# The last graph layer of four: its linear products kept in SBUF up to the output, a degree factor moved into the edge sums

## The chip, the cores and the metric

The kernel is one program on one core of a Trainium2 chip. The metric is the device time of that program in microseconds, from launch to the last output row in memory. Five instruction streams run side by side on the core and meet only through semaphores: TensorE (PE), VectorE (DVE), ScalarE (ACT), GpSimd (POOL) and SyncE (SP), which here does nothing but issue DMA transfers.

## What is computed

Four graph layers on 10,000 nodes of 512 features and 5,000 edges sorted by target: a GIN layer, a SAGE layer, a two-layer attention block and a GCN layer. Each is followed by a residual sum and a layer normalisation. The change is in the fourth, apart from two small tables that are made earlier.

```python
def _gcn_conv(x, edge_index, W, b):
    xw = x @ W.T
    deg = ...                      # edges into the node, plus its own loop
    dinv = rsqrt(deg)
    norm = dinv[row] * dinv[col]   # source times target
    out = segment_sum(norm[:, None] * xw[row], col)
    return out + b

identity = x
h = _gcn_conv(x, edge_index, W, b)
h = _batch_norm(h, gamma, beta)    # mean and variance of each feature over all nodes
h = gelu(h)
x3_out = h + identity
x = _layernorm(x + x3_out, axis=-1)
```

The batch norm needs statistics over all nodes, so no row of the output can be made before the last row of `h` has been seen. Since both `dinv[col]` and the loop belong to the target, the input of the product for node n is `dinv[n] * (sum over its edges of dinv[src] * x[src] + dinv[n] * x[n])`.

## The kernel before

The nodes are padded to 10,240 and taken in 20 groups of 512, each group as four subtiles of 128 rows. The program is a row of stages. At the end of each stage all five engines meet at a barrier (`Kernel.run`, lines 284 to 288), so that a stage lasts as long as its slowest engine and its slowest awaited transfer. The last four stages are:

1. **Edge sums** (`edge_sum_stage`, line 952). The 40 tiles of 128 edges are gathered by POOL (line 987), multiplied on PE by a mask whose entries carry the source's factor (lines 1033 and 1056), and copied out of PSUM by ACT into one of three buffers (line 1047, or line 1045 where `out_scale` is given). SP stores each tile's sums and picks two of their rows for sums that run across tiles (lines 1005 to 1007). ACT waits until the buffer's three transfers of three tiles ago have landed.
2. **Linear stage** (`linear_stage(kn, "gcn")`, line 1660). SP loads the group's rows of x3 into `l_x`, POOL gathers its edge sums into `l_z`. DVE makes `x * dinv + sum` (line 1753) and multiplies the result by `dinv` once more (line 1758). PE turns it feature by feature (line 1820), ACT and DVE split it into two float16 parts (lines 1789 and 1765), and PE makes four products `mm[m]` of 12 matmuls each with the weights' two parts (`split_product`, lines 320 to 322). ACT adds the bias (line 1801) into `l_h`, DVE takes batch norm statistics of it (line 1779), and SP stores the group's `l_h`, 1 MB, in the scratch tensor `h` in memory (line 1710). The turns of the next group stand ahead of products m = 2 and m = 3 (`turns`, line 1671), with two PSUM banks for them.
3. **Coefficients** (`norm_coefficients_stage`, line 1844): aggregates the statistics (line 1856) into one scale and shift for each feature.
4. **Batch norm stage** (`batch_norm_stage(kn, "gcn")`, line 1876). SP loads the group's `h` again into `b_h` (line 1924), 1 MB, and its x3 into `b_x` (line 1928), 1 MB. ACT applies scale, shift and Gelu (line 2023), PE turns the result back to rows (line 2067), DVE forms `2 * x + turned` (line 1984) with layer norm statistics (lines 1425 and 1428), POOL makes the reciprocal root (lines 1434 and 1437), DVE applies it into `b_o` (line 1445), and SP stores 1 MB of output rows (line 1935). All buffers are in pairs.

The loops of stages 2 and 4 are hardware loops over pairs of groups, with the last pair written out behind the loop (`in_pairs`, line 131). Stage 1 is straight-line code. The order on each engine is the order in which the code is written. The order on SP in stage 4 is, for each group, load of h, load of x, wait for the group's output rows, store.

Whoever reads the code: `kn.w_hi` and `kn.w_lo` hold all layers' weights in SBUF, 13 units of 2,048 float16 columns and a few more, in each of 128 partitions. The last unit (`W_GCN`) is the GCN layer's. The others, the masks `kn.apart` and two bias tiles have been read for the last time when stage 2 begins.

## Time and profile before

| | us |
|---|---|
| median of three runs | 4247.26 |
| fastest and slowest of them | 4243.65 and 4253.40 |
| the profiled execution, its own time | 4247.18 |
| the profiled execution, its span | 4245.5 |
| edge sums of the last layer, first to last instruction | 3627 to 3723 |
| linear stage | 3725 to 4012.5 |
| coefficients | 4016 to 4020.6 |
| batch norm stage | 4020.7 to 4245.5 |

The span is from the first to the last instruction of the profiled execution; 1.68 us of its own time lie outside it. Over the whole program PE is busy 84%, PE's weight loads 51%, DVE 51%, ACT 34% and POOL 34% of the span. These shares hide that the stages have different limits: PE is busy 94% of the linear stage and 32% of the batch norm stage. The reader should take times of the trace as microseconds from the span's start, and "idle" as time in which an engine stood before the named instruction.

### The profile page before, as it was taken

Reading aid. Unit: us, or ns where it says so; the run is one execution under the profiler, and the core shown is the slowest. Engines: PE = TensorE matmul, PEld = TensorE weight load, DVE = VectorE, ACT = ScalarE, POOL = GpSimd, SP = SyncE. Lnnn points to the kernel's source line nnn. Section 1 sums busy time; section 2 is a strip of 40 time slices with the busy share of each in tenths; the row PEclk is TensorE's granted clock in tenths of the full one; section 3 lists DMA queues with packets and bytes.
Section 4 is the critical chain, followed back from the end, with each engine's and each line's share of the span. In section 5 each row is a group of like instructions: output and inputs, shape, how many; then the busy total and the mean of one; then the engine's idle time right before and its main releaser. Section 6 shows DMA issues by size and latency. Waiting matters only on the chain. (4 is left out here: it accounts for less than half of the span.)

```text
span 4245.5 us, 59057 instructions
## 1 busy us (share of the span) xinstructions
PE 3572.1 (84%) x20056; PEld 2145.6 (51%) x20056; DVE 2165.2 (51%) x4085; ACT 1429.8 (34%) x2512; POOL 1455.5 (34%) x1188
## 2 busy tenths in 40 slices
PE   4589994599997999987599999998859999679733
PEld 3134441255554777765366666666635555234422
DVE  7167776433333444446643424213757887057576
ACT  1333333222222444344233323222534443323332
POOL 2455543322211222243433333213446665333111
PEclk7799996799998999999799999999979999789955
DMA  1767766543433556577876676744867675657587
GB/s 66 225 176 199 200 168 229 176 141 119 136 111 143 209 209 225 191 219 220 244 204 201 196 205 196 207 110 149 265 225 268 248 267 185 207 199 238 203 278 276
DMA packets 554428, 841.83 MB, mean 198 GB/s; under 512 B 288134, under 2 KB 288134, under 8 KB 552272
## 3 DMA queue, kind: packets, MB, share of 16 engines
q1 hardware_dynamic: 487120, 619.31, 44.4%
q0 software_dynamic: 67200, 221.25, 17.7%
q8 instruction: 47, 0.77, 0.1%
q14 instruction: 61, 0.50, 0.0%
HBM read 491.80 MB, written 284.56 MB: 183 GB/s over the span
## 5 line engine op out<-in xcount | busy, mean ns | idle before, releaser
L321 PE MATMUL bank<-w_lo,t_r_hi 128*128 128x344 f16 (+1 forms) x2560 | 837.1, 327 | 0.0
L322 PE MATMUL bank<-w_hi,t_r_hi 128*128 128x344 f16 (+1 forms) x2560 | 836.9, 327 | 0.0
L320 PE MATMUL bank<-w_hi,w_lo 128*128 128x344 f16 (+1 forms) x1280 | 418.7, 327 | 30.7 <-DMA w_lo<-g_row_lo 30.7
L2237 DVE SCALAR_TENSOR_TENSOR t_z<-w_lo,t_z 128x256 f32<-128x256 f32 x320 | 205.9, 704 | 440.3 <-DMA w_lo<-h 437.8
L320 PE MATMUL bank<-l_z_hi,w_lo 128*128 128x512 f16 x960 | 365.3, 381 | 1.5 <-DVE l_z_lo L1765 1.5
L321 PE MATMUL bank<-l_z_lo,w_hi 128*128 128x512 f16 x960 | 365.3, 380 | 0.0
L322 PE MATMUL bank<-l_z_hi,w_hi 128*128 128x512 f16 x960 | 365.0, 380 | 0.0
L2211 POOL TENSOR_TENSOR t_row_lo<-t_r,t_row_hi 128x1024 f16<-128x1024 f32 x80 | 181.3, 2267 | 517.0 <-ACT t_row_hi L2258 516.8
L1456 POOL DMA_INDIRECT l_z<-sum,slot_i x160 | 160.6, 1004 | 519.5 <-PE bank L1820 436.7
L320 PE MATMUL bank<-w_hi 128*128 128x344 f16 x960 | 297.7, 310 | 45.5 <-DMA w_hi<-t_row_lo 45.5
L322 PEld LDWEIGHTS bank<-w_hi,t_r_hi 128*128 128x128 f16 x2560 | 250.9, 98 | 168.3 <-issue 0.3
L321 PEld LDWEIGHTS bank<-w_lo,t_r_hi 128*128 128x128 f16 x2560 | 250.8, 98 | 162.1 <-issue 0.2
L1779 DVE BATCH_NORM_STATS2 bn_stats<-l_h 128x512 f32 (+2 forms) x160 | 107.1, 679 | 415.0 <-ACT l_h L1801 365.0
L320 PE MATMUL bank<-w_hi,b_z_lo 128*128 128x344 f16 x960 | 297.2, 310 | 0.0
L321 PE MATMUL bank<-w_lo,b_z_hi 128*128 128x344 f16 x960 | 297.1, 309 | 0.0
L322 PE MATMUL bank<-w_hi,b_z_hi 128*128 128x344 f16 x960 | 297.0, 309 | 0.0
L1056 PE MATMUL bank<-e_rows,e_lhs 128*128 128x512 f32 x240 | 164.9, 819 | 146.2 <-ACT e_out L1045 49.7
L2269 ACT ACTIVATE w_hi<-bank 128x344 f32<-128x344 f32 x240 | 109.1, 456 | 516.6 <-PE bank L322 516.6
L1801 ACT ACTIVATE l_h<-bank,vec 128x512 f32<-128x512 f32 x160 | 109.9, 687 | 507.4 <-PE bank L322 471.3
L2067 PE MATMUL bank<-ident,b_h 128*128 128x128 f32 x640 | 115.6, 349 | 169.3 <-ACT b_h L2023 167.2
L320 PE MATMUL bank<-w_hi,t_r_lo 128*128 128x512 f16 x640 | 242.8, 379 | 0.0
L2413 POOL TENSOR_TENSOR t_r_lo<-t_r,t_r_hi 128x512 f16<-128x512 f32 x160 | 196.3, 1235 | 96.4 <-ACT t_r_hi L2481 89.6
(277 smaller groups left out, 7031.7 us busy)
## 6 DMA issues: line engine op xcount, KB each, us to landing
w_lo<-h SPq DMA_DIRECT2D x160, 512.0 KB
h<-b_wide SPq DMA_DIRECT2D x80, 516.0 KB, 3.0
...
```

The costliest lines, as they stand in the source:

```text
L320: pe.matmul(out, s_lo, m_hi, start=(k == 0), stop=False)
L321: pe.matmul(out, s_hi, m_lo, start=False, stop=False)
L322: mm = pe.matmul(out, s_hi, m_hi, start=False, stop=last)
L1056: pe.matmul(total[t % 2][:], lhs[t % L][:], rows[t % W][:], start=True, stop=True).then_inc(summed.sem, 1)
L1456: pool.indirect_dma_start(out, None, sums, bass.IndirectOffsetOnAxis(ap=kn.slot_i[:, g * S + s:g * S + s + 1], axis=0), bounds_check=kn.d. ...
L1779: v.bn_stats(kn.bn_stats[:, m, ds(g * 6, 6)], h[u][:, m, 0:real]).then_inc(seen.sem, 1)
L1801: act.activation(h[u][:, m, :], mm[m][:], ACT.Identity, scale=UNSCALE, bias=kn.vec[:, bias + m:bias + m + 1]).then_inc(h_done.sem, 1)
L2067: ins = pe.transpose(tp[u][s][:, m * P:(m + 1) * P], h[u][:, m, s * P:(s + 1) * P], kn.ident[:])
L2211: nc.gpsimd.tensor_tensor(row_lo[:, s, :], r_f[s % 2][:], row_hi[:, s, :], ALU.subtract)\
L2237: ins = v.scalar_tensor_tensor(out=z[u][:, s, cols], in0=hrow[:, s, cols], scalar=z[u][:, s, HC + h:HC + h + 1], in1=z[u][:, s, cols], op0 ...
L2269: act.activation(wide[s % 2][:, third * THIRD:(third + 1) * THIRD], mm[s % 2][third], ACT.Copy, scale=UNSCALE).then_inc(wide_done.sem, 1)
L2413: g_.tensor_tensor(r_lo[:, u, k, :], r_f[k % 2][:], r_hi[:, u, k, :], ALU.subtract)\
```

## The change

The batch norm stage of the last layer no longer reads its input back from memory. A new class `Held` names 80 places of 128 by 512 float32 in SBUF, four for each group: 48 in the room of the used weights, 5 in the masks', 2 in the bias tiles', 17 new buffers, and for the last two groups the two input buffers `l_x`. `gcn_stage` takes the place of `linear_stage(kn, "gcn")`. ACT writes each product with its bias to its place, and nothing is stored. It has four PSUM banks for turned rows, all four turns of the next group stand ahead of product m = 1, and DVE scales the input of group g + 2 ahead of the statistics of product m = 2 of group g. DVE's second pass over the input is gone. For this the edge sums of the last layer are multiplied by the target's factor while they leave PSUM (`out_scale`, and `rim_dinv` for sums that cross tiles), and the node's own row by the squared factor `node_scale`. DVE makes the two degrees in the setup, and POOL makes three small tables of them at the end of the second layer's linear stage.

`output_stage` takes the place of `batch_norm_stage(kn, "gcn")`. ACT applies Gelu in place. Only x3 is loaded, four groups ahead, into four own buffers and then into the room of held groups that have been turned and read (`held.whole`). DVE's sum is written over x in place, and ACT instead of DVE applies the layer norm, in place, with a shift that POOL makes in two more small operations. The output is stored from there. Both new stages are straight-line code.

```diff
@@ -709,11 +714,13 @@
         dve.wait_ge(own, n)
         n = st.mark(v.tensor_scalar(alike[:], alike[:], 1.0, None, ALU.add))
         dve.wait_ge(own, n)
+        v.tensor_tensor(kn.dst_dinv[:], alike[:], inside[:], ALU.add).then_inc(tables.degrees.sem, 1)
         st.mark(v.reciprocal(kn.mean_scale[:], alike[:]))
         dve.wait_ge(products.sem, products.at(RIM_COUNTED))
         st.mark(v.tensor_scalar(rim_f[0:T, 4:5], rim_count_ps, -1.0, float(T * P), ALU.mult, ALU.add))
         n = st.sig.at(st.first + st.n)
         dve.wait_ge(own, n)
+        v.tensor_scalar(kn.rim_dinv[0:T, :], rim_f[0:T, 4:5], 1.0, None, ALU.add).then_inc(tables.degrees.sem, 1)
         st.mark(v.reciprocal(kn.rim_mean_scale[0:T, :], rim_f[0:T, 4:5]))
         v.memset(kn.bn_stats[:], 0.0)
         slots(dve)
@@ -1738,7 +1745,13 @@
         if sage:
             pool.wait_ge(dinv_in.sem, dinv_in.at(16 * d.tiles))
             nc.gpsimd.tensor_scalar(kn.src_dinv_neg[:], kn.src_dinv[:], -1.0, None, ALU.mult).then_inc(negated.sem, 1)
-            pool.wait_ge(negated.sem, negated.at(1))
+            nc.gpsimd.tensor_tensor(kn.dst_dinv[:], kn.dst_dinv[:], kn.minus_half[:, 0:d.tiles], ALU.pow)\
+                .then_inc(negated.sem, 1)
+            nc.gpsimd.tensor_tensor(kn.rim_dinv[0:d.tiles, :], kn.rim_dinv[0:d.tiles, :],
+                                    kn.minus_half[0:d.tiles, 0:1], ALU.pow).then_inc(negated.sem, 1)
+            nc.gpsimd.tensor_tensor(kn.node_scale[:], kn.node_dinv[:], kn.node_dinv[:], ALU.mult)\
+                .then_inc(negated.sem, 1)
+            pool.wait_ge(negated.sem, negated.at(4))
 
     def vector(dve):
         v = nc.vector
+class Held:
+    def __init__(self, kn, mem):
+        d = kn.d
+        room = []
+        for w in (kn.w_hi, kn.w_lo):
+            free = w[:, 0:kn.unit_at(W_GCN)].bitcast(F32)
+            room += [free[:, n * D:(n + 1) * D] for n in range(kn.unit_at(W_GCN) // (2 * D))]
+        free = kn.apart[:].rearrange("p t q -> p (t q)").bitcast(F32)
+        room += [free[:, n * D:(n + 1) * D] for n in range(d.tiles * P // (2 * D))]
+        room += [kn.gin_b2[:], kn.fc_b[:]]
+        self.x = [kn.buffer(mem, f"l_x{u}", [P, S, D], F32) for u in range(2)]
+        room += [kn.buffer(mem, f"held{n}", [P, D], F32)[:] for n in range((d.groups - 2) * 4 - len(room))]
+        room = room[:(d.groups - 2) * 4] + [self.x[u][:, m, :] for u in range(2) for m in range(4)]
+        self.rows = [room[g * 4:g * 4 + 4] for g in range(d.groups)]
+        self.whole = [w[:, n * 8 * D:(n + 1) * 8 * D].bitcast(F32).rearrange("p (s c) -> p s c", s=S)
+                      for w in (kn.w_hi, kn.w_lo) for n in range(kn.unit_at(W_GCN) // (8 * D))]
+def gcn_stage(kn, held):
...
+    tp = [kn.bank[n] for n in (0, 1, 6, 7)]
+    mm = [kn.bank[2 + n] for n in range(4)]
...
+    def sync(sp):
+        for g in range(G):
+            i, u = divmod(g, 2)
+            if g >= 2:
+                sp.wait_ge(z_ready.sem, z_ready.at((g - 1) * S))
+            sp.dma_start(x[u][:], node_rows(dram["x3"], i, u)).then_inc(x_in[u].sem, 16)
+    def gpsimd(pool):
+        for g in range(G):
+            i, u = divmod(g, 2)
+            if g >= 2:
+                pool.wait_ge(turned.sem, turned.at((g - 1) * 4))
+            for s in range(S):
+                gather_sums(kn, pool, z[u][:, s, :], dram["sum"], g, s, sum_in[u])
+    def vector(dve):
+        v = nc.vector
+        def scale(g):
+            i, u = divmod(g, 2)
+            dve.wait_ge(x_in[u].sem, x_in[u].at(i * 16 + 16))
+            dve.wait_ge(sum_in[u].sem, sum_in[u].at(16 * S * (i + 1)))
+            for s in range(S):
+                own = kn.node_scale[:, g * S + s:g * S + s + 1]
+                v.scalar_tensor_tensor(out=z[u][:, s, :], in0=x[u][:, s, :], scalar=own,
+                                       in1=z[u][:, s, :], op0=ALU.mult, op1=ALU.add).then_inc(z_ready.sem, 1)
+        def low_parts(g):
+            u = g % 2
+            for k in range(4):
+                dve.wait_ge(hi_done.sem, hi_done.at(g * 4 + k + 1))
+                v.scalar_tensor_tensor(out=z_lo[u][:, k, :], in0=tp[k][:], scalar=A_SCALE, in1=z_hi[u][:, k, :],
+                                       op0=ALU.mult, op1=ALU.subtract).then_inc(lo_done.sem, 1)
+        scale(0)
+        low_parts(0)
+        scale(1)
+        for g in range(G):
+            for m in range(4):
+                if m == 1 and g + 1 < G:
+                    low_parts(g + 1)
+                if m == 2 and g + 2 < G:
+                    scale(g + 2)
+                dve.wait_ge(h_done.sem, h_done.at(g * 4 + m + 1))
+                v.bn_stats(kn.bn_stats[:, m, g * 6:(g + 1) * 6], held.rows[g][m][:, 0:real(g)]).then_inc(seen.sem, 1)
+        dve.wait_ge(seen.sem, seen.at(4 * G))
+    def scalar(act):
+        def high_parts(g):
+            u = g % 2
+            for k in range(4):
+                act.wait_ge(turned.sem, turned.at(g * 4 + k + 1))
+                act.activation(z_hi[u][:, k, :], tp[k][:], ACT.Copy, scale=A_SCALE).then_inc(hi_done.sem, 1)
+        high_parts(0)
+        for g in range(G):
+            for m in range(4):
+                if g + 1 < G and m == 1:
+                    high_parts(g + 1)
+                own = held.rows[g][m]
+                act.wait_ge(mid.sem, mid.at(g * 4 + m + 1))
+                act.activation(own, mm[m][:], ACT.Identity, scale=UNSCALE,
+                               bias=kn.vec[:, V_GCN_B + m:V_GCN_B + m + 1]).then_inc(h_done.sem, 1)
+    def tensor(pe):
+        def turn(g):
+            u = g % 2
+            pe.wait_ge(z_ready.sem, z_ready.at(g * S + S))
+            for k in range(4):
+                pe.wait_ge(lo_done.sem, lo_done.at((g - 1) * 4 + k + 1))
+                for s in range(S):
+                    ins = pe.transpose(tp[k][:, s * P:(s + 1) * P], z[u][:, s, k * P:(k + 1) * P], kn.ident[:])
+                ins.then_inc(turned.sem, 1)
+        turn(0)
+        for g in range(G):
+            u = g % 2
+            pe.wait_ge(lo_done.sem, lo_done.at(g * 4 + 4))
+            for m in range(4):
+                if g + 1 < G and m == 1:
+                    turn(g + 1)
+                pe.wait_ge(h_done.sem, h_done.at((g - 1) * 4 + m + 1))
...
...
+def output_stage(kn, held):
...
+    own = [kn.buffer(mem, f"o_x{b}", [P, S, D], F32)[:] for b in range(B)]
+    x = (own + held.whole + own)[:B + len(held.whole)] + own
...
+    tp = [kn.bank[0:4], kn.bank[4:8]]
...
+    def sync(sp):
+        def load(g):
+            if g >= B:
+                sp.wait_ge(y_done.sem, y_done.at((g - B) * S + S))
+            if g >= B + len(held.whole):
+                sp.wait_ge(first_stored.sem, first_stored.at(16 * B))
+            sp.dma_start(x[g], node_rows(dram["x3"], *divmod(g, 2))).then_inc(x_in[g % B].sem, 16)
...
+            sp.wait_ge(rows_out.sem, rows_out.at(g * S + S))
+            sp.dma_start(node_rows(dram["out"], *divmod(g, 2)), x[g])\
+                .then_inc((first_stored if g < B else stored).sem, 16)
+        sp.wait_ge(first_stored.sem, first_stored.at(16 * B))
+        sp.wait_ge(stored.sem, stored.at(16 * (G - B)))
+    def gpsimd(pool):
+        for g in range(G):
+            i, u = divmod(g, 2)
+            if g >= 2:
+                pool.wait_ge(rows_out.sem, rows_out.at((g - 1) * S))
+            norm.pool(pool, i, u)
+            pool.wait_ge(norm.rstd.sem, norm.rstd.at(g * 2 + 2))
+            nc.gpsimd.tensor_tensor(shift[:, u, :], norm.moments[:, u, :, 0], norm.power[:, u, :], ALU.mult)\
+                .then_inc(shifted.sem, 1)
+            pool.wait_ge(shifted.sem, shifted.at(g * 2 + 1))
+            nc.gpsimd.tensor_scalar(shift[:, u, :], shift[:, u, :], -1.0, None, ALU.mult).then_inc(shifted.sem, 1)
+    def vector(dve):
+        v = nc.vector
+        for g in range(G):
+            i, u = divmod(g, 2)
+            b = g % B
+            dve.wait_ge(x_in[b].sem, x_in[b].at(16 * (g // B + 1)))
+            if g >= 2:
+                dve.wait_ge(rows_out.sem, rows_out.at((g - 1) * S))
+            for s in range(S):
+                dve.wait_ge(rows_turned.sem, rows_turned.at(g * S + s + 1))
+                v.scalar_tensor_tensor(out=x[g][:, s, :], in0=x[g][:, s, :], scalar=2.0, in1=tp[u][s][:],
+                                       op0=ALU.mult, op1=ALU.add).then_inc(y_done.sem, 1)
+                dve.wait_ge(y_done.sem, y_done.at(g * S + s + 1))
+                norm.moments_of(dve, x[g][:, s, :], s, i, u)
+    def scalar(act):
+        def apply(g):
+            for m in range(4):
+                own = held.rows[g][m]
+                act.activation(own, own, ACT.Gelu, scale=kn.bn_scale[:, m:m + 1],
+                               bias=kn.bn_shift[:, m:m + 1]).then_inc(f_done.sem, 1)
+        apply(0)
+        apply(1)
+        for g in range(G):
+            u = g % 2
+            if g + 2 < G:
+                apply(g + 2)
+            act.wait_ge(shifted.sem, shifted.at(g * 2 + 2))
+            for s in range(S):
+                act.activation(x[g][:, s, :], x[g][:, s, :], ACT.Identity, scale=norm.power[:, u, s:s + 1],
+                               bias=shift[:, u, s:s + 1]).then_inc(rows_out.sem, 1)
+    def tensor(pe):
+        for g in range(G):
+            u = g % 2
+            pe.wait_ge(f_done.sem, f_done.at(g * 4 + 4))
+            for s in range(S):
+                pe.wait_ge(y_done.sem, y_done.at((g - 2) * S + s + 1))
+                for m in range(4):
+                    ins = pe.transpose(tp[u][s][:, m * P:(m + 1) * P], held.rows[g][m][:, s * P:(s + 1) * P],
+                                       kn.ident[:])
+                ins.then_inc(rows_turned.sem, 1)
...
 def graph_layers_kernel(nc, nodes, edges, io):
     d = Dims(nodes, edges)
     dram = dict(io)
@@ -2578,10 +2837,12 @@
         kn.add(edge_attention_stage(kn, dram["h2"]))
         kn.add(gat_stage(kn, 2))
         with ExitStack() as mem:
-            kn.add(edge_sum_stage(kn, mem, dram["x3"], (kn.src_dinv, kn.src_dinv_neg), None, None))
-        kn.add(linear_stage(kn, "gcn"))
-        kn.add(norm_coefficients_stage(kn, V_GCN_G, V_GCN_BETA))
-        kn.add(batch_norm_stage(kn, "gcn"))
+            kn.add(edge_sum_stage(kn, mem, dram["x3"], (kn.src_dinv, kn.src_dinv_neg), kn.dst_dinv, kn.rim_dinv))
+        with ExitStack() as mem:
+            held = Held(kn, mem)
+            kn.add(gcn_stage(kn, held))
+            kn.add(norm_coefficients_stage(kn, V_GCN_G, V_GCN_BETA))
+            kn.add(output_stage(kn, held))
         kn.run()
```

DVE's rows of the last two groups in the linear stage, before, behind the loop. `l_z` is the input, `l_z_lo` its low part, `bn_stats` the statistics, and `l_h_247` and `l_h_248` the two groups' products:

```order
L1753 SCALAR_TENSOR_TENSOR l_z_244<-l_x_242,node_dinv,l_z_244 128x512 x4
L1758 TENSOR_SCALAR l_z_244<-l_z_244,node_dinv 128x512 x4
L1779 BN_STATS bn_stats<-l_h_247 128x6 x2
L1765 SCALAR_TENSOR_TENSOR l_z_lo<-bank,l_z_hi 128x512 x2
L1779 BN_STATS bn_stats<-l_h_247 128x6
L1765 SCALAR_TENSOR_TENSOR l_z_lo<-bank,l_z_hi 128x512 x2
L1779 BN_STATS bn_stats<-l_h_247 128x6
L1779 BN_STATS bn_stats<-l_h_248 128x6 x4
```

The same engine now, two groups in the middle of the new stage:

```order
L2633 SCALAR_TENSOR_TENSOR l_z_lo_265<-bank,l_z_hi_263 128x512 x4
L2646 BN_STATS bn_stats<-w_hi 128x6
L2626 SCALAR_TENSOR_TENSOR l_z_260<-l_x_241,node_scale,l_z_260 128x512 x4
L2646 BN_STATS bn_stats<-w_hi 128x6 x3
L2633 SCALAR_TENSOR_TENSOR l_z_lo_264<-bank,l_z_hi_262 128x512 x4
L2646 BN_STATS bn_stats<-w_hi 128x6
L2626 SCALAR_TENSOR_TENSOR l_z_261<-l_x_242,node_scale,l_z_261 128x512 x4
L2646 BN_STATS bn_stats<-w_hi 128x6 x3
```

The scaling of a group stood directly ahead of the low parts of the same group, in two passes. It is now one pass, and the low parts of another group and four statistics stand between a group's scaling and its own low parts.

ACT's rows at the start of the last stage, before (`b_h` is the reloaded h). The branch closes the loop:

```order
L2023 ACT_TABLE_LOAD
L2023 ACTIVATE b_h_252<-b_h_252,bn_shift,bn_scale 128x512 x4
L2023 ACTIVATE b_h_253<-b_h_253,bn_shift,bn_scale 128x512 x4
L134 REGISTER_ALU
L134 COMPARE_AND_BRANCH
```

And now, where `w_hi` is room of held products, and `o_x_269` and `o_x_270` are the first two groups' output rows:

```order
L2767 ACT_TABLE_LOAD
L2767 ACTIVATE w_hi<-w_hi,bn_shift,bn_scale 128x512 x12
L2778 ACTIVATE o_x_269<-o_x_269,o_shift,n_power 128x512 x4
L2767 ACTIVATE w_hi<-w_hi,bn_shift,bn_scale 128x512 x4
L2778 ACTIVATE o_x_270<-o_x_270,o_shift,n_power 128x512 x4
```

Gelu of three groups now stands ahead of the first layer norm on ACT, and one group's Gelu stands between each two layer norms. There is one table load in front of all of them.

## Rows read from the trace of the kernel before

**Rows 1.** Busy time by window; columns: window, length, PE, PEld, DVE, ACT, POOL, PEclk, DMA, GB/s.
```profile
3627.00:3720.00 93.00, 55.43 (x81) 17.77 (x82) 0.00 (x0) 38.91 (x80) 39.98 (x40) 0.74 0.75 239
3747.50:4012.50 265.00, 247.28 (x1264) 127.51 (x1264) 180.67 (x309) 93.96 (x156) 72.41 (x72) 0.99 0.65 218
4020.70:4245.50 224.80, 71.15 (x320) 63.86 (x320) 158.34 (x320) 70.08 (x89) 30.97 (x40) 0.58 0.81 280
...
4000.00:4011.00 11.00, 11.00 (x52) 4.80 (x49) 2.03 (x4) 2.75 (x4) 0.00 (x0) 1.00 0.25 95
...
3450.00:3500.00 50.00, 50.00 (x265) 26.66 (x263) 40.27 (x66) 20.29 (x32) 31.28 (x30) 1.00 0.72 260
```

**Rows 2.** Waits in the last stage, 4050 to 4200: total us, times, longest.
```profile
ACT b_h L2023 <- DMA b_h<-h: 102.7, 14, 13.1
```

**Rows 3.** Waits of PE in the linear stage, 3760 to 4011.
```profile
PE bank L1820 <- DVE l_z L1758: 16.0, 18, 0.9
```

**Rows 4.** Timeline of PE around one of these waits; start, duration, what, idle before.
```profile
3965.95 0.38 PE L322 MATMUL bank<-l_z_hi,w_hi 128*128 128x512 f16 x1
3967.25 1.09 PE L1820 MATMUL bank<-ident,l_z 128*128 128x128 f32 x8 [0.92 <-DVE l_z L1758]
```

**Rows 5.** Timeline of DVE: the second pass, in the first group and at that wait.
```profile
3739.98 1.68 DVE L1758 TENSOR_SCALAR l_z<-l_z,node_dinv 128x512 f32<-128x512 f32 x4
...
3965.43 1.67 DVE L1758 TENSOR_SCALAR l_z<-l_z,node_dinv 128x512 f32<-128x512 f32 x4
```

**Rows 6.** Timeline of DVE at the end of the linear stage.
```profile
4011.81 0.45 DVE L1779 BATCH_NORM_STATS2 bn_stats<-l_h 128x6 f32<-128x272 f32 x1 [2.15 <-ACT l_h L1801]
4016.12 2.36 DVE L1856 BATCH_NORM_AGGREGATE c_mv<-bn_stats 128x2 f32<-128x120 f32 x4 [3.87 <-SPq L287]
```

**Rows 7.** Timeline at the start of the last stage.
```profile
4020.82 1.28 ACT L2023 ACT_TABLE_LOAD   x1 [9.05 <-DVEq L287]
...
4026.19 2.93 ACT L2023 ACTIVATE b_h<-b_h,bn_shift,bn_scale 128x512 f32<-128x512 f32 x4 [4.08 <-DMA b_h<-h]
4029.25 3.67 PE L2067 MATMUL bank<-ident,b_h 128*128 128x128 f32 x16 [18.20 <-ACT b_h L2023]
4030.50 0.69 DVE L1984 SCALAR_TENSOR_TENSOR b_y<-b_x,bank 128x512 f32<-128x512 f32 x1 [9.90 <-PE bank L2067]
```

**Rows 8.** Timeline of DVE: subtiles of one group in the last stage.
```profile
4165.39 0.69 DVE L1984 SCALAR_TENSOR_TENSOR b_y<-b_x,bank 128x512 f32<-128x512 f32 x1 [3.72 <-PE bank L2067]
...
4167.06 0.69 DVE L1984 SCALAR_TENSOR_TENSOR b_y<-b_x,bank 128x512 f32<-128x512 f32 x1
...
4172.18 1.92 DVE L1445 TENSOR_SCALAR b_o<-b_y,n_moments,n_power 128x512 f32<-128x512 f32 x4
```

**Rows 9.** DMA in the last stage: its mean over 4050 to 4200, and one window.
```profile
DMA packets 22262, 44.21 MB, mean 295 GB/s; under 512 B 676, under 2 KB 676, under 8 KB 22262
...
4051.00:4062.00 11.00, 3.59 (x16) 3.27 (x16) 6.62 (x15) 4.21 (x5) 1.75 (x2) 0.55 1.03 366
```

**Rows 10.** Timeline at the end of the program.
```profile
4235.40 0.18 DVE L1428 BATCH_NORM_AGGREGATE n_moments<-n_stats 128x2 f32<-128x6 f32 x1
...
4236.19 1.27 POOL L1437 TENSOR_TENSOR n_power<-n_power,minus_half 128x4 f32<-128x4 f32 x1
4237.58 1.91 DVE L1445 TENSOR_SCALAR b_o<-b_y,n_moments,n_power 128x512 f32<-128x512 f32 x4 [0.15 <-POOL n_power L1437]
```

**Rows 11.** Lines 1045 and 1047 (min, median, max ns), and waits in 3627 to 3722.
```profile
L1045 ACT ACTIVATE e_out<-bank,mean_scale x40: 675/687/688, 686.0 to 788.3; 128x512 f32<-128x512 f32 x40
...
L1047 ACT COPY e_out<-bank x80: 572/585/586, 110.2 to 3714.3; 128x512 f32<-128x512 f32 x80
...
ACT e_out L1047 <- DMA e_last<-e_out: 30.7, 23, 3.6
```

**Rows 12.** POOL: costliest groups, and its timeline around the SAGE layer's end.
```profile
L531 POOL TENSOR_TENSOR node_dinv<-degree,minus_half 128x80 f32<-128x80 f32 x1 | 13.3, 13319 | 0.1
...
1312.03 0.23 POOL L1868 TENSOR_SCALAR c_rstd<-c_mv 128x4 f32<-128x4 f32 x1 [75.86 <-DVE c_mv L1856]
```

54 lines of the change are left out of this document (53 added, 1 removed).

## The prediction, made before the changed kernel ran

> **What bounds the kernel now.** I read the windows by stage first, since the change touches only the last 620 us of 4245.5 [rows 1]. In the linear stage (265 us from its first product to its end) PE is busy 247 us at a granted clock of 0.99, so PE sets the pace there. In the last stage (224.8 us) PE is busy 71 us, DVE 158, ACT 70, and the DMA engines 0.81 of the time at 280 GB/s. No engine is full there, so I went to the waits. ACT stood 102.7 of 150 us until the reload of h had landed, on 14 of 14 groups [rows 2]. The loop closes through a pair of buffers: the next h is requested when PE has turned the last one, and 3 MB a group (h, x, output) must pass. This costs 224.8 / 20 = 11.2 us a group. In the linear stage the one wait of PE is for DVE's second pass over the input [rows 3].
>
> **Linear stage, steady part.** PE stood 16.0 us in 18 waits, 0.89 us each [rows 3]. In the timeline the last product before such a wait starts at 3965.95 and the turn at 3967.25 [rows 4], while products follow each other every 11.00 / 52 = 0.21 us when nothing waits [rows 1]. So the step takes 1.30 us instead of 0.21, of which 0.92 is counted as idle; about 0.17 more hides under the modelled end of the product. The second pass (1.67 us [rows 5]) ends just before the turn starts. The change removes it and also puts the whole scaling one group earlier on DVE, so the wait should vanish, not shrink: 18 x (0.89 + 0.17) = **19.1 us**. What is late next? A group then takes PE some 12.1 us. DVE's work in it is four scalings, four low parts and four statistics, at about 0.7 us each 8.4 us, ACT's eight operations of 0.6 to 0.7 us some 5.2 us. The new scaling of group g + 2 waits for gathers that POOL issues once group g has been turned, more than a group earlier. If they were late, DVE would hold back statistics, which nothing on PE needs. The four turn banks are freed by low parts of a group before. Nothing is left for PE to wait on. The share of dense work rises; a stretch in which PE was busy 50.00 of 50 us kept a clock of 1.00 [rows 1], so I take no loss of clock.
>
> **Linear stage, its two ends.** The first group's second pass, 1.68 us, lies between its input and the first turn [rows 5]: **1.7 us**. Four banks in place of two may add some tenths, left out. At the end, the last statistics finish at 4012.26, and the aggregation starts only at 4016.12, after 3.87 us of idle that SP's queue ended, the last store of h [rows 6]. That store is gone. A barrier alone takes 0.2 us or so (the last stage's table load starts within that of the coefficients' end), so **3.6 us**. The stores of h elsewhere in the stage cost nothing and give nothing back.
>
> **Last stage, start.** Before, the stage's start at 4020.7 leads over the first landing of h to ACT at 4026.19, PE at 4029.25 and DVE at 4030.50 [rows 7]. Now ACT loads its table (1.28 us, to 4022.10) and has its input at once: four Gelus, 2.93 us, to 4025.05; PE 0.13 later; DVE 1.25 after PE, at 4026.4. The first x is now the first transfer asked for and should land as h did, by 4026.2, just hidden. First DVE operation: 5.7 us after the start of the stage.
>
> **Last stage, pace.** DVE per subtile: 4167.06 - 4165.39 = 1.67 us for sum, statistics and aggregation, with its waits between [rows 8]; four make 6.68 us. The application, 1.92 us a group, leaves DVE. Against this stand: ACT with four Gelus (2.93 us, [rows 7]) and four layer norm applications. The last form is not in the trace for SBUF input; it costs at most what Gelu costs in place, 2.93, and at least what DVE took, 1.92. I take 2.9, near Gelu, since it runs on the same engine with the same two vector operands. ACT is then busy 5.9 us of 6.68. Does its latency fit? After DVE ends a group, POOL's chain takes 1.9 us as before (4235.58 to 4237.46 [rows 10]) and 0.6 us for two more small operations (one such takes 0.23 [rows 12]); ACT's application ends 5.5 us after DVE's end, its Gelu for three groups on 8.4 us after, and PE's turn of 3.7 us at 12.1 us, when DVE needs it at 13.4. It fits with about 1 us over. PE's turns themselves take 3.7 of 6.7 us. DMA moves 2 MB (2.10 million bytes) a group instead of 3: in 6.68 us that is 314 GB/s. The stage's mean was 295 GB/s with ACT waiting for it, but a window of 11 us ran at 366 [rows 9], which would need 5.7 us a group. So DVE becomes the bound: 20 x 6.68 = **133.6 us**.
>
> On DMA, the Trainium skill (DMA: Bandwidth & Descriptors, Specifications) gives a limit of about 358 GB/s between memory and one core. By that figure a group would need at least an estimated 5.9 us, and the sum would stay as it is. The trace's 366 GB/s over 11 us lies slightly above it.
>
> **Last stage, end.** Before, from the last aggregation's end (4235.58) to the span's end (4245.5) passed 9.9 us [rows 10]. POOL's two operations add 0.6, ACT's application in place of DVE's 1.0: 11.5 us. The whole stage is 5.7 + 133.6 + 11.5 = 150.8 us against 224.8: **74.0 us** less.
>
> **Edge sums.** The copy out of PSUM with a factor took 0.687 us against 0.585 without [rows 11], on 40 tiles. If each were on the path, 4.1 us; if none, 0. It cannot gain. SP's queue (three transfers a tile) sets much of the pace, while ACT waited for a landing 23 times [rows 11]; behind such a wait the 0.1 us counts, but the three buffers share it. I take **+1.5 us**, nearer the lower end.
>
> **What should cost nothing.** DVE's two new operations in the setup are on tables of 40 columns, some 0.2 us each, beside edge sums. POOL's power over 80 columns took 13.3 us [rows 12], so the two new powers and a product may take 7 to 8 us. They stand behind POOL's last gather in the SAGE layer, where POOL then idles 75.9 us until the stage's end [rows 12]. Without that cover they would cost those 8 us.
>
> **Sum.** 4247.18 (the profiled execution, 1.68 outside its span) - 19.1 - 1.7 - 3.6 - 74.0 + 1.5 = 4150.3. The median of the three runs is 0.08 higher. I say **4150 us**. Its own range is 4142 to 4156: DVE's subtile may take 1.63 us (3 us less over 80), the edge sums 0 to 4.1 us, the tail and the starts 2 us either way.
>
> **Rivals.**
>
> *DMA sets the last stage's pace.* If loads and stores interleave no better than before, at 295 GB/s [rows 9], a group takes 7.1 us and the stage 8.4 us more: **4159 us**. For it: loads and stores of 1 MB alternate on one queue, and the required 314 GB/s is above the mean of before. Against it: that mean contains times in which nothing was asked for, and loads run four groups ahead. Chance 0.14.
>
> *ACT sets it.* The application now shares an engine and a latency loop with Gelu. If Gelu and the application needed different tables, two loads of 1.28 us would be added: 5.9 + 2.6 = 8.5 us a group, 36 us more, **4186 us**. For it: the trace shows a table load again and again in the last stage. Against it: the order of the changed kernel has a single one, ahead of all groups. A milder form, an application that waits 0.5 us a group longer than I count, gives 4160. Chance 0.07 together.
>
> *The linear stage keeps its wait.* With all turns ahead of one product, high parts, low parts and turns form a chain in one place, and PE may wait there as long as it did: 4169 us. Against it: PE has three products, 7.8 us, behind the turns, and the chain behind them is 2 us long. Chance 0.04.
>
> *Straight-line code starves the engines: slower than before.* Both stages lose their loops. PE gets 960 products and 320 turns in the linear stage as fresh code, with their weight loads. If fetching it made each of these 1,280 pairs wait, the gain of 97 us would be gone at 0.076 us a pair, a pace of 0.29 us instead of 0.21. At 0.1 us a pair the time is 4150 + 128 = **4278 us**. Against it: the last two groups before are already behind the loop, and ran at 0.21 us [rows 1]; that is only 200 pairs or so, so longer streams are not shown. Chance 0.03.
>
> The Trainium skill (Runtime: NRT & Kernel Launch, Instruction fetch mechanics) says that the sequencer prefetches code in order in blocks of 16 KiB, mostly hidden, and that taken branches are what breaks it. By that rule this rival's cost is nothing. No row here shows a long dense stream of new code.
>
> **Chances and range.** Forecast 0.70, DMA 0.14, ACT 0.07, linear wait 0.04, slower 0.03, and 0.02 that some other cost eats the gain to within 0.2% (8 us), which is about what a measurement of this kernel can tell from no change. A range of 4135 to 4170 takes in the forecast, the DMA case, the mild ACT case and the kept linear wait, and some room below for starts that overlap better and subtiles of 1.63 us. Faster by over 0.2%: 0.95; within: 0.02; slower: 0.03.
>
> **What would show it.** In the changed profile: no wait of PE for DVE in the linear stage, and 12.1 us a group there; the aggregation within 0.5 us of the last statistics; DVE in the last stage with 1.67 us a subtile and hardly any idle, ACT waiting for POOL's shift and not for DMA; one table load; DMA near 310 GB/s; the last stage near 151 us, the edge sums 1 to 2 us longer. It would be wrong if DVE's sum waits for `o_x` or `w_hi` transfers (DMA), or for turns that wait for Gelu (ACT), or if PE's products space out beyond 0.22 us (code).

## The result, and the profile after

The changed kernel takes **4139.28 us**, the median of 4 runs (4137.12 to 4144.01), against 4247.23 (4243.65 to 4253.4, 4 runs) for the kernel before on the same chip. The ratio is 0.9746 (95% interval 0.973 to 0.9761): 108 us less. Two later sets of five runs gave medians of 4143.16 and 4140.17, so a single median is good to some 2 to 4 us. The forecast of 4150 with the range 4135 to 4170 held; the gain was 7 to 11 us larger than foretold. The prediction's narrower range for its own forecast, 4142 to 4156, did not take in 4139.28.

The windows of the changed kernel by stage (window, length, busy time of PE, PEld, DVE, ACT, POOL, granted clock, DMA share, GB/s) are: the input of the linear stage, its steady part, the coefficients, the last stage. They answer to [rows 1].

```profile
3721.60:3741.20 19.60, 3.65 (x16) 3.27 (x16) 5.56 (x9) 2.39 (x4) 8.64 (x9) 0.53 0.83 267
3741.20:3982.60 241.40, 240.66 (x1264) 127.56 (x1264) 148.11 (x231) 92.06 (x156) 77.29 (x72) 1.00 0.49 153
3982.60:3987.80 5.20, 0.00 (x0) 0.00 (x0) 3.29 (x8) 1.29 (x2) 1.29 (x2) 0.81 0.01 3
3987.80:4135.10 147.30, 67.79 (x320) 60.93 (x320) 117.29 (x240) 115.08 (x160) 33.37 (x80) 0.59 0.84 285
```

From the first product on PE is busy 240.66 of 241.40 us. Before, it was busy 247.28 of 265.00. The last stage takes 147.3 us instead of 224.8, and ACT is now as full there as DVE. The waits of PE between 3700 and 3960 answer to [rows 3]; the columns are total us, times, longest:

```profile
PE bank L2673 <- DVE l_z L2626: 17.7, 1, 17.7
...
PE bank L324 <- DVE l_z_lo L2633: 1.4, 1, 1.4
```

Both stand at the start of the stage, ahead of the first turn and the first product. No wait of PE follows until the stage's end at 3982.6. The 18 waits of 0.9 us in [rows 3] are gone. The timeline at the seam of the stages (start, duration, what, idle before) answers to [rows 6, 7]:

```profile
3982.63 0.44 DVE L2646 BATCH_NORM_STATS2 bn_stats<-l_x 128x6 f32<-128x272 f32 x1 [2.15 <-ACT l_x L2663]
3983.22 2.36 DVE L1869 BATCH_NORM_AGGREGATE c_mv<-bn_stats 128x2 f32<-128x120 f32 x4
3983.23 1.28 ACT L2767 ACT_TABLE_LOAD   x1 [0.64 <-PEq L291]
...
3987.79 8.57 ACT L2767 ACTIVATE w_hi<-w_hi,bn_shift,bn_scale 128x512 f32<-128x512 f32 x12 [3.28 <-DVEq L291]
3990.82 7.53 PE L2788 MATMUL bank<-ident,w_hi 128*128 128x128 f32 x44 [8.95 <-ACT w_hi L2767]
3993.47 0.69 DVE L2758 SCALAR_TENSOR_TENSOR o_x<-o_x,bank 128x512 f32<-128x512 f32 x1 [5.75 <-DMA o_x<-x]
```

The aggregation follows the last statistics after 0.15 us (3983.22 less 3983.07), where DVE had stood 3.87 us. ACT's table load now comes right behind the linear stage's barrier, 4.5 us ahead of the first Gelu, so it hides under the coefficients; the forecast had it inside the last stage. The first sum still starts 5.7 us after the stage, since its input x now lands last: 3993.47 less 3987.79.

DVE's subtiles in the last stage (answer to [rows 8]) and the waits of 3995 to 4120 (answer to [rows 2]):

```profile
4041.20 0.65 DVE L2758 SCALAR_TENSOR_TENSOR w_hi<-w_hi,bank 128x512 f32<-128x512 f32 x1
4041.88 0.69 DVE L1432 BATCH_NORM_STATS2 n_stats<-w_hi 128x6 f32<-128x512 f32 x1
4042.72 0.18 DVE L1435 BATCH_NORM_AGGREGATE n_moments<-n_stats 128x2 f32<-128x6 f32 x1
4042.82 0.66 DVE L2758 SCALAR_TENSOR_TENSOR w_hi<-w_hi,bank 128x512 f32<-128x512 f32 x1
```

```profile
ACT o_x L2778 <- POOL o_shift L2746: 10.0, 6, 5.8
ACT w_hi L2778 <- POOL o_shift L2746: 5.0, 6, 0.8
ACT w_lo L2778 <- POOL o_shift L2746: 5.0, 6, 0.8
...
DVE n_moments L1435 <- DVE n_stats L1432: 0.3, 2, 0.2
```

No engine waits for a reloaded h or for x. ACT waits 0.8 us a group for POOL's shift, and DVE stands for nothing but its own last result: a period of 1.62 to 1.66 us a subtile. So DVE is the bound, as forecast. Of its 1.62 us only 0.65 + 0.69 + 0.18 = 1.52 are busy as counted; the step from the start of the statistics to the start of the aggregation takes 0.84 us.

### The profile page after: what moved, and what is told of

Its sections match the earlier page's. It is cut to its first block and busy times, and to the rows that moved or that the text cites. A ratio compares the mean times of both kernels' runs of the same rounds, so it can differ in the third digit from the quotient of the medians.

```text
span 4135.1 us, 57582 instructions
## 1 busy us (share of the span) xinstructions
PE 3554.7 (86%) x20056; PEld 2138.1 (52%) x20056; DVE 2089.7 (51%) x3927; ACT 1479.1 (36%) x2584; POOL 1476.6 (36%) x1231
## 5 line engine op out<-in xcount | busy, mean ns | idle before, releaser
L1792 DVE BATCH_NORM_STATS2 bn_stats<-l_h 128x512 f32 (+2 forms) x80 | 54.5, 682 | 337.2 <-ACT l_h L1814 299.6
L2491 ACT ACTIVATE t_r<-bank,vec_scaled 128x512 f32<-128x512 f32 x160 | 109.7, 685 | 293.3 <-PE bank L2522 241.6
L1463 POOL DMA_INDIRECT t_z<-sum_gat,slot_i x160 | 166.2, 1039 | 122.1 <-SPq L291 79.2
```

Of the source, the lines that this page charges most:

```text
L1463: pool.indirect_dma_start(out, None, sums, bass.IndirectOffsetOnAxis(ap=kn.slot_i[:, g * S + s:g * S + s + 1], axis=0), bounds_check=kn.d. ...
L1792: v.bn_stats(kn.bn_stats[:, m, ds(g * 6, 6)], h[u][:, m, 0:real]).then_inc(seen.sem, 1)
L2491: act.activation(r_f[k % 2][:], tp[k % 4][:], ACT.Relu, scale=A_SCALE, bias=kn.vec_scaled[:, bias + k:bias + k + 1]).then_inc(r_done.sem, 1)
```

## The experiments

Each kernel ran beside the kernel before on the same chip (medians there 4244.43, 4244.93 and 4248.45). "Path" is read from each trace: first product to last statistics for the linear stage, first sum to last aggregation for the last stage.

| kernel | median us | ratio, 95% interval |
|---|---|---|
| before, with the degree factors alone | 4219.85 | 0.9938 [0.9921, 0.9955] |
| before, two stages in straight-line code | 4243.8 | 0.9995 [0.9985, 1.0004] |
| changed, second pass put back early | 4142.85 | 0.9755 [0.9733, 0.9777] |
| changed, no factor in the edge sums | 4141.13 | 0.9754 [0.9741, 0.9767] |
| changed, DVE applies the layer norm | 4173.44 | 0.9832 [0.9814, 0.985] |
| changed, h stored again | 4144.2 | 0.9758 [0.9744, 0.9771] |
| changed, a third megabyte a group | 4163.56 | 0.9805 [0.979, 0.982] |
| changed, DVE's order interleaved | 4119.77 and 4120.69 | 0.97 [0.9685, 0.9715] |
| changed itself, twice more | 4143.16 and 4140.17 | 0.9757 [0.9744, 0.9771] |

Where two medians stand, the interval is that of the first.

**One part alone: the degree factors.** To the kernel before, with its loops, its h in memory and its reload:

```diff
-                dinv = kn.node_dinv[:, ds(i * (2 * S) + u * S + s, 1)]
+                dinv = kn.node_scale[:, ds(i * (2 * S) + u * S + s, 1)]
...
-            for s in range(S):
-                dinv = kn.node_dinv[:, ds(i * (2 * S) + u * S + s, 1)]
-                v.tensor_scalar(z[u][:, s, :], z[u][:, s, :], dinv, None, ALU.mult)\
-                    .then_inc(z_ready[u].sem, 1)
```

> The kernel before with one part of the change: the target's factor goes into the edge sums, the node's own row gets the squared factor, DVE's second pass is gone. Loops, the store of h and its reload stay. Theory A (the second pass, directly ahead of the turn, was all that PE waited for): 19.1 us in the steady part and 1.7 us at the start go, 1.5 us come in the edge sums, so 4228 us, and no wait of PE for DVE in the linear stage. Theory B (the wait goes only because the whole scaling is now a group earlier): most of the 19 us stays, 4240 to 4247 us.

Measured: 24.6 us less than before (4244.43 to 4219.85), where Theory A's terms came to 19.3; the interval allows 19 to 34. Between the stage's first product and its end PE waits for nobody. Its path takes 243.9 us against 264.5; 0.9 us of that are four slow products fewer (see "The slow clock" below). The scaling to the first product is 1.7 us shorter (10.58 to 8.87), as the single pass says. The rest of the program keeps its pace: 204.6 us in the last stage against 205.1. So some 22 to 25 of the 108 us came with the factors alone, and they need neither the new order nor the held products.

**Straight-line code alone.** In the kernel before, both stages' loops are written out and nothing else changes:

```diff
+def all_pairs(eng, n, body):
+    for i in range(n // 2):
+        for u in range(2):
+            body(i, u, i == n // 2 - 1 and u == 1)
...
+    pairs = in_pairs if sage else all_pairs
...
-        in_pairs(pe, G, group)
+        pairs(pe, G, group)
```

> The kernel before with the last layer's linear stage and batch norm stage written out group by group instead of as loops over pairs; nothing else differs. Theory A (loops and fetching cost nothing that counts, all of the gain is in what waits): 4245 to 4249 us. Theory B (part of the gain that went beyond the forecast comes from the lost register instructions, seen as 1.645 us a subtile on DVE instead of 1.67, and as products at full clock from the start): 4238 to 4244 us. Theory C (new code starves PE): 4260 us or more.

Measured: 4243.8 against 4244.43, no difference told apart (0.9985 to 1.0004, which still allows 6 us less). The median cannot choose between Theory A and Theory B, whose ranges meet at 4244 to 4245. The waits of this kernel, of PE in its linear stage and of ACT in its last stage:

```profile
PE bank L1828 <- DVE l_z L1766: 12.8, 18, 0.7
...
ACT b_h L2032 <- DMA b_h<-h: 140.8, 19, 12.9
```

Straight-line code costs nothing, which removes the rival that ended slower. It gains little either: each wait of PE falls from 0.89 to 0.71 us. The second pass and the turn behind it, in this kernel:

```profile
3965.24 1.67 DVE L1766 TENSOR_SCALAR l_z<-l_z,node_dinv 128x512 f32<-128x512 f32 x4
3966.97 1.09 PE L1828 MATMUL bank<-ident,l_z 128*128 128x128 f32 x8 [0.72 <-DVE l_z L1766]
```

The pass takes 1.67 us as in the loop, although its factor now stands at a fixed address. What shrinks is the way from one engine to the next: the turn starts 0.06 us behind the pass (3966.97 less 3966.91) where it took 0.15 before (3967.25 less 3967.10, [rows 4, 5]), and the statistics start 0.72 us behind the start of ACT's bias (3961.11 to 3961.83) where it was 0.82 (3961.19 to 3962.01). In the last stage a subtile takes 1.63 us instead of 1.67, and the sum 664 ns on the mean instead of 687. The profile of before has the same 1.63 us in the first and the last group, which stand outside its loop:

```profile
4230.61 0.66 DVE L1984 SCALAR_TENSOR_TENSOR b_y<-b_x,bank 128x512 f32<-128x512 f32 x1
4232.24 0.66 DVE L1984 SCALAR_TENSOR_TENSOR b_y<-b_x,bank 128x512 f32<-128x512 f32 x1
```

That sum has the same fixed operands in both kernels, so the 0.04 us belong to the loop; by what in it, no run shows. ACT still waits for h at every group, so loops were not the last stage's limit. The linear path is 4.5 us shorter (264.5 to 260.0, 1.5 of it by seven slow products fewer) and the last stage's 2.1 us (205.1 to 203.0). The span is only 2.0 us shorter, since the edge sums' first copy came 5.0 us later in this profile, which is scatter.

**The second pass back, a group early.** In the changed kernel:

```diff
+    z_first = take("z_first", S * G)
...
-                                       in1=z[u][:, s, :], op0=ALU.mult, op1=ALU.add).then_inc(z_ready.sem, 1)
+                                       in1=z[u][:, s, :], op0=ALU.mult, op1=ALU.add).then_inc(z_first.sem, 1)
+            dve.wait_ge(z_first.sem, z_first.at(g * S + S))
+            for s in range(S):
+                v.tensor_scalar(z[u][:, s, :], z[u][:, s, :], kn.ones[:, 0:1], None, ALU.mult)\
+                    .then_inc(z_ready.sem, 1)
```

> The changed kernel with the second pass put back on DVE (a multiplication by ones), right behind the first, so a group earlier than before the change. Theory A (the place of the pass made the wait, and DVE has room): only the first group's 1.7 us come back, 4141 us, no wait of PE for DVE later on. Theory B (DVE's load in the linear stage made the wait): 12 to 20 us come back, 4151 to 4159 us.

Measured: 4142.85, the time of the changed kernel within its scatter. The 1.67 us of DVE work in each group is back, and PE waits for it only in the first group, where the way from scaling to product grows by 1.7 us (7.90 to 9.60). From there to the end of the stage PE has no wait for DVE but the one for the first low part, as in the changed kernel. The wait ahead of the first turn:

```profile
PE bank L2678 <- DVE l_z L2631: 19.2, 1, 19.2
```

Together with the first experiment: removing the pass is enough, and in the new stage moving it is enough. The wait came from the place of the pass, between PE and its next turn, not from DVE's load.

**No factor in the edge sums.** This kernel leaves out the target's degree factor, so its sums are the source-scaled ones, and its copies out of PSUM are plain.

```diff
-            kn.add(edge_sum_stage(kn, mem, dram["x3"], (kn.src_dinv, kn.src_dinv_neg), kn.dst_dinv, kn.rim_dinv))
+            kn.add(edge_sum_stage(kn, mem, dram["x3"], (kn.src_dinv, kn.src_dinv_neg), None, None))
```

> The changed kernel without the target's factor in the last edge sums: they are copied out of PSUM plainly, as before the change (this leaves out part of the computation). Theory A (the longer copy, 0.687 against 0.585 us, counts only behind late landings): 1 to 2 us less than the changed kernel beside it. Theory B (SP's queue and the landings set the stage, the copy is hidden): no difference, within 1 us. Theory C (each copy is on the path): 4 us less.

Measured: 4141.13 against 4143.16 for the changed kernel beside it, intervals 0.9741 to 0.9767 and 0.9744 to 0.9771: no difference told apart. From the stage's first copy to its end the traces give 84.1 us here, 85.0 and 84.4 in the two kernels before without the factor, and 82.8 to 86.3 in ten with it. The 0.1 us on each of 40 copies is there (687 against 584 ns in the groups of ACT) and hides: ACT stands for landings in either kernel, 30.7 us before [rows 11] and in the changed kernel

```profile
ACT e_out L1052 <- DMA e_last<-e_out: 29.5, 32, 2.0
```

**DVE applies the layer norm again.** In the changed kernel, with POOL's two operations for the shift left out:

```diff
+            if g:
+                norm.apply(dve, x[g - 1], x[g - 1], *divmod(g - 1, 2), rows_out)
...
-            for s in range(S):
-                act.activation(x[g][:, s, :], x[g][:, s, :], ACT.Identity, scale=norm.power[:, u, s:s + 1],
-                               bias=shift[:, u, s:s + 1]).then_inc(rows_out.sem, 1)
```

> The changed kernel, but DVE applies the layer norm again, in place, one group behind its sums; POOL's two small operations for the shift are gone. Theory A (DVE sets the pace of the last stage at 6.58 us a group): each group takes 1.92 us more, 20 groups 38 us, the tail 1.6 us less, so 4176 us. Theory B (DMA or the loop through POOL and ACT sets it, and DVE is only near it): 4139 to 4155 us.

Measured: 4173.44, 30 us above the changed kernel. DVE's rows:

```profile
4060.18 0.69 DVE L2752 SCALAR_TENSOR_TENSOR w_hi<-w_hi,bank 128x512 f32<-128x512 f32 x1
...
4066.72 1.88 DVE L1452 TENSOR_SCALAR w_hi<-w_hi,n_moments,n_power 128x512 f32<-128x512 f32 x4
4068.70 0.69 DVE L2752 SCALAR_TENSOR_TENSOR w_hi<-w_hi,bank 128x512 f32<-128x512 f32 x1
```

A group takes 4068.70 - 4060.18 = 8.52 us, four subtiles of 1.64 (4060.18 to 4066.72) and 1.98 for the application, and the stage's path is 167.0 us against 131.7. DVE is the bound on both sides of this edit. It also splits the last stage's gain: of 73.4 us on the path from the first sum to the last aggregation (205.1 to 131.7), 38.1 come with h kept in SBUF and the stage written for it (205.1 to 167.0) and 35.3 with the move of the application to ACT.

**h stored again.** The 21 MB of h are written as well, from the held rows, with nobody reading them:

```diff
+    def store(sp, g):
+        for m in range(4):
+            sp.wait_ge(h_done.sem, h_done.at(g * 4 + m + 1))
+            sp.dma_start(dram["h"][m, :, g * GROUP:(g + 1) * GROUP], held.rows[g][m]).then_inc(kept.sem, 16)
...
```

> This kernel is the changed one with one removed transfer put back: the 21 MB of h are also stored from the held rows during the last linear stage, four transfers of 256 KB a group (nobody reads them). Nothing else moves; the last stage still works from SBUF. Theory A (the stores themselves cost nothing while they run, since a group's product takes 12 us and 1 MB more fits in it; only the last one shows, because the stage ends when it has landed): the path of the linear stage keeps its 241 to 244 us, the stretch from the last statistics to the end of the coefficients grows from 4.6 to about 8.4 us as in the kernel before, and the time is 3.6 us above the changed kernel run beside it. Rival B (the stores compete with the loads or with the edge stage's tail for the DMA queues): waits of PE for DVE come back and the time is 10 us or more above. Rival C (the stage's end has other cover now): no difference, within 1.5 us.

Measured: 4144.2 (4139.93 to 4147.81) against 4140.17 (4138.2 to 4150.62) for the changed kernel beside it. Their intervals overlap, and these medians alone cannot tell a cost of 1.5 us from one of 3.6. In the trace the path of the linear stage is 242.1 us, as without the stores (241.9), although DMA moves 238 GB/s there instead of 153:

```profile
3742.33:3984.43 242.10, 240.88 (x1264) 127.51 (x1264) 148.23 (x232) 92.15 (x156) 80.01 (x72) 1.00 0.77 238
```

```profile
3986.03 2.36 DVE L1869 BATCH_NORM_AGGREGATE c_mv<-bn_stats 128x2 f32<-128x120 f32 x4 [1.60 <-SPq L291]
```

The stores cost nothing while they run. Only the last one shows, and it costs 1.5 us (6.10 against 4.65 from the last statistics to the coefficients' end), not the 3.6 expected. The likely reason, not tried by itself, is that the last piece is 256 KB, asked for when its own product is ready, where the kernel before sent the whole 1 MB at once. Theory A in kind, at less than half its size.

**A third megabyte a group.** Each group's output rows are stored a second time, into a scratch tensor that is no longer read:

```diff
+                sp.wait_ge(again.sem, again.at(16 * 12))
...
+            sp.dma_start(node_rows(dram["x1"], *divmod(g, 2)), x[g]).then_inc(again.sem, 16)
...
```

The first of these lines holds the loads of the last four groups until the second stores of twelve groups have landed.

> The changed kernel with a third megabyte a group in the last stage: each group's output rows are stored a second time, into scratch memory, and no compute engine waits for that. Theory A (before the change the bytes themselves were the limit; at 366 GB/s three megabytes take 8.6 us): a group takes 8.6 us or more instead of 6.6, 4175 to 4190 us. Theory B (the bytes had room, and the loss was the loop through a pair of buffers): under 4155 us.

Measured: 4163.56, between the theories. DMA over 4010 to 4130, in 40 slices of 3 us, first this kernel and then the changed one (3995 to 4120):

```profile
GB/s 345 321 298 405 403 402 403 361 401 408 404 402 388 408 410 409 405 408 402 408 412 407 403 403 406 408 404 410 407 393 366 43 117 371 391 382 401 409 407 410
DMA packets 22840, 45.42 MB, mean 378 GB/s; under 512 B 687, under 2 KB 687, under 8 KB 22835
```

```profile
GB/s 387 341 299 173 281 358 267 360 269 362 286 347 306 342 296 362 300 306 342 317 329 275 359 284 345 279 352 282 358 275 359 295 350 305 345 351 6 290 46 250
DMA packets 18906, 37.61 MB, mean 301 GB/s; under 512 B 572, under 2 KB 572, under 8 KB 18900
```

Here bytes are the limit, at some 405 GB/s: 3.15 million bytes then take 7.8 us a group. DVE begins with four groups of x ahead and keeps 6.58 us a group up to the twelfth; the later groups take 7.0 to 8.5. So its path is 144.9 us (7.25 a group) and the stores run late: 19.4 us pass from the last aggregation to the end instead of 9.9. One group takes 11.4 us, and that is the added wait's doing (the 43 and 117 GB/s above):

```profile
SPq L2724 <- DMA x<-w_lo: 10.8, 1, 10.8
4111.73 0.69 DVE L2762 SCALAR_TENSOR_TENSOR o_x<-o_x,bank 128x512 f32<-128x512 f32 x1 [4.73 <-DMA o_x<-x]
```

So some 4 to 5 of the 20 us over the changed kernel (4143.16) belong to that wait and not to the bytes. The kernel before moved the same 3 MB in a longer period. The 11.2 us of the prediction hold the stage's two ends; from the first sum of the first group (4030.50, [rows 7]) to that of the twentieth it is 19 periods of 10.4 us:

```profile
4228.95 0.69 DVE L1984 SCALAR_TENSOR_TENSOR b_y<-b_x,bank 128x512 f32<-128x512 f32 x1 [3.50 <-PE bank L2067]
```

At the 405 GB/s seen here, 7.8 of these 10.4 us would be bytes. The other 2.6 us are put down to the closed loop through a pair of buffers: request, landing, Gelu, turn, next request. That is argued and not shown by a run: the kernel before loads two megabytes and stores one, this one loads one and stores two, and no kernel with the reload and more buffers for it was run.

**DVE's order interleaved.** The sum of subtile s+1 stands ahead of the statistics of s, and those ahead of the aggregation of s-1. The arithmetic is the same. POOL's chain and the statistics use new semaphores, and one small thing is gone: the changed kernel increments a semaphore between each subtile's statistics and its aggregation (`settle`, called from the layer norm's helper), and this one does not.

```diff
+            for n in range(S + 2):
+                if n < S:
+                    s = n
+                    dve.wait_ge(rows_turned.sem, rows_turned.at(g * S + s + 1))
+                    v.scalar_tensor_tensor(out=x[g][:, s, :], in0=x[g][:, s, :], scalar=2.0, in1=tp[u][s][:],
+                                           op0=ALU.mult, op1=ALU.add).then_inc(y_done.sem, 1)
+                if 1 <= n <= S:
+                    s = n - 1
+                    dve.wait_ge(y_done.sem, y_done.at(g * S + s + 1))
+                    v.bn_stats(norm.stats[:, u, s, :], x[g][:, s, :]).then_inc(ln_stats.sem, 1)
+                if n >= 2:
+                    s = n - 2
+                    dve.wait_ge(ln_stats.sem, ln_stats.at(g * S + s + 1))
+                    v.bn_aggr(norm.moments[:, u, s, :], norm.stats[:, u, s, :]).then_inc(ln_moments.sem, 1)
...
```

> The changed kernel with another order on DVE in the last stage: the sum of subtile s + 1, the statistics of s and the aggregation of s - 1 take turns, so that none waits for the result just ahead of it. Theory A (DVE sets the pace by its waits for its own results too): a subtile takes 1.35 to 1.45 us, and the next limit takes over, ACT with 5.85 us of work a group or DMA with 5.7: 5.9 to 6.1 us a group, 4125 to 4131 us. Theory B (DVE's operations alone set it, the waits were overlapped): 4136 us or more.

> The changed kernel with the interleaved order on DVE in the last stage once more (for each group: the sum of subtile s+1, the statistics of s, the aggregate of s-1), beside the changed kernel itself. Theory A (DVE's waits for its own results were the rest of its time a group): about 23 us under the changed kernel, 4115 to 4124. Theory B (the first result came from a good set of runs): less than 15 us under it.

Measured: 4119.77 (the changed kernel beside it: 4143.16) and, the second time, 4120.69 (beside 4140.17): 20 to 23 us less than the changed kernel, 3% under the kernel before, the fastest version here. DVE and ACT over one group:

```profile
4044.18 0.69 DVE L2772 BATCH_NORM_STATS2 n_stats<-w_hi 128x6 f32<-128x512 f32 x1
4044.78 0.67 DVE L2767 SCALAR_TENSOR_TENSOR w_hi<-w_hi,bank 128x512 f32<-128x512 f32 x1
4045.37 0.69 DVE L2772 BATCH_NORM_STATS2 n_stats<-w_hi 128x6 f32<-128x512 f32 x1
4045.97 0.17 DVE L2776 BATCH_NORM_AGGREGATE n_moments<-n_stats 128x2 f32<-128x6 f32 x1
4046.05 0.65 DVE L2767 SCALAR_TENSOR_TENSOR w_hi<-w_hi,bank 128x512 f32<-128x512 f32 x1
...
4048.62 1.28 DVE L2767 SCALAR_TENSOR_TENSOR w_hi<-w_hi,bank 128x512 f32<-128x512 f32 x2 [0.43 <-PE bank L2803]
...
4042.79 2.92 ACT L2782 ACTIVATE w_lo<-w_lo,bn_shift,bn_scale 128x512 f32<-128x512 f32 x4
4045.61 2.92 ACT L2793 ACTIVATE w_hi<-w_hi,o_shift,n_power 128x512 f32<-128x512 f32 x4
4048.43 2.92 ACT L2782 ACTIVATE w_lo<-w_lo,bn_shift,bn_scale 128x512 f32<-128x512 f32 x4
```

A subtile takes 4046.05 - 4044.78 = 1.27 us instead of 1.64: sum to statistics 0.59, statistics to the next sum 0.68 with the aggregation in it. A group takes 5.64 us (4042.79 to 4048.43), and ACT's eight operations fill it without a gap, 0.705 us each, while DVE stands 0.43 us a group for PE. The bound has passed to ACT. The 0.37 us a subtile have three main parts. The statistics start 0.59 instead of 0.68 us behind the sum ahead of them. In the changed kernel the increment stands 0.73 us behind the start of the statistics, where the next operation here starts 0.60 behind them, and the aggregation follows 0.11 us behind the increment. The increments on DVE in the changed kernel, 80 of them in this stage:

```profile
L128 DVEq EVENT_SEMAPHORE  x320: 21/21/21, 243.3 to 4124.9; - x160
```

So up to 0.11 of the 0.37 us may be the increment's and not the order's; no run separates them. By an estimate from these rows it hardly changes the time: DVE needs 5.64 - 0.43 = 5.21 us a group here, and four increments at 0.11 would make it 5.65, beside ACT's 5.64.

The Trainium skill (VectorE: DVE Perf Modes, The DRAIN you can't avoid) finds for a chain of copies on DVE that semaphores between them cost nothing. Here they do cost: a wait for the operation just ahead delays the statistics by 0.09 us, and the aggregation's by 0.13 us before its increment.

## Why the prediction was right, point by point

The spans differ by 4245.5 - 4135.1 = 110.4 us, and the prediction's terms sum to 96.9. The 13.5 us between them, from the two traces (the last stage's start is counted from the coefficients' end):

| step of the prediction | foretold | in the trace |
|---|---|---|
| linear stage, steady wait | -19.1 | -19.6 |
| second pass and banks at the start | -1.7 | -2.7 |
| products at the slow clock at the start | none | -3.0 |
| last h store | -3.6 | -3.7 |
| start of the last stage, to the first sum | 5.7 us long | 5.8 |
| its pace, 20 groups | 133.6 us long | 131.7 |
| its end | 11.5 us long | 9.9 |
| edge sums | +1.5 | -2.2 |
| first input of the linear stage | 0 | -0.6 |
| all stages before | 0 | -1.1 |

**Linear wait.** Right in mechanism and size, and shown twice (the factors alone; the second pass put back early). The rival that it would stay fell: PE has no wait after its first product. In 19.6 the slow products below are taken out (264.46 - 241.86 - 3.0).

**The start.** The pass gave its 1.7 us. The four banks, "some tenths, left out", gave 1.0: the kernel with factors alone needs 8.87 us from scaling to product, the changed one 7.90. Straight-line code alone gave 0.1 of it (10.58 to 10.49).

**The slow clock.** A gain that was not foretold and is not the change's. The first products of the stage run at a granted clock of 0.50 (1.2 GHz), 0.43 us apart, and then at 1.00 (2.4 GHz), 0.216 apart. In the profile before these were 14 products, in the changed kernel's own none, and in another profile of the same changed kernel nine, of which these rows show the last two and the two that follow:

```profile
3742.59 0.63 PE L325 MATMUL bank<-l_z_lo,w_hi 128*128 128x512 f16 x1
3743.02 0.57 PE L326 MATMUL bank<-l_z_hi,w_hi 128*128 128x512 f16 x1
3743.43 0.38 PE L324 MATMUL bank<-l_z_hi,w_lo 128*128 128x512 f16 x1
3743.64 0.38 PE L325 MATMUL bank<-l_z_lo,w_hi 128*128 128x512 f16 x1
```

Each costs 0.214 us more, so two profiles of one kernel can differ by some 2 to 3 us there. In the ten other profiles the count was 0 four times, 7 once, 9 twice and 10 three times. PE had stood idle for most of the 19 us before the first product in all of them alike. What sets the count is not shown.

**The last stage.** The 5.7 us at its start came right by another path than foretold. The table load did not stand in it, so the first turn starts at 3990.82 and the sum, 1.25 us behind it, could have started at 3992.07, 4.3 us after the stage's start. But the sum waits for x, which the forecast had just hidden, until 3993.47. That the term fits is luck in part.

The bound was named rightly, DVE with 1.67 us a subtile. The term was 0.025 us too large, over 80 subtiles the 1.9 us: 1.67 was read from a group inside the loop, and the groups outside it, in the same trace, have 1.63, as the straight-line kernel has throughout. The end came 1.6 us sooner than foretold: the last store landed 4.9 us behind ACT's end (4127.26 + 2.92 to 4135.1), where before it had taken 6.0 behind DVE's (4237.58 + 1.91 to 4245.5, [rows 10]), and POOL's chain took 2.1 us instead of 2.6. The DMA rival was priced by 295 GB/s; DMA did not become the bound at 301 GB/s, and the third megabyte shows why: it can give 405. The limit of about 358 GB/s that the prediction cited from the Trainium skill (DMA: Bandwidth & Descriptors, Specifications) did not hold for this core, which moved 378 GB/s as a mean over 120 us. The ACT rivals fell with the single table load, but ACT, with a wait of only 0.8 us a group, was near to being the bound.

**Edge sums.** This is the step that failed, though by little. The prediction had the slower copy count behind some of ACT's waits for landings and took +1.5. The kernel without the factor is not told apart from the one with it. The stage's length varies by 3.5 us between profiles whatever the copy, so the -2.2 is scatter, and the term was nothing within that. It was a small one: it made 1.5 of the 13.5 us.

**Straight-line code.** The rival that would have made the kernel slower was tried by itself and cost nothing (0.9985 to 1.0004). PE's 1,280 pairs ran at 0.216 us a product through the whole stream. The rule of the Trainium skill that the prediction cited (Runtime: NRT & Kernel Launch, Instruction fetch mechanics) agrees: no stall shows.

**What stays open.** The remaining drift of 1.1 us in front of the edge sums is within what profiles of one kernel show: the stage's first copy came at 3633.7, 3637.0 and 3640.2 in three profiles of the changed kernel. The forecast was high by 7 to 11 us against the medians; of the 13.5 us between the spans some 7 (3.0 of slow products, 2.2 of edge sums, 1.7 ahead of them and in the first input) are scatter of two single profiles. The rest, some 6.5, are mis-sized terms: the pace 1.9, the end 1.6, the edge sums 1.5, the start of the linear stage 1.0, its wait 0.5. All of them err to the same side. What the loop through a pair of buffers cost before, as against the bytes, stays an inference too.
